# ScalarE applies the first norm four slots later in a software-pipelined vision tower

## The reference, cut to what matters

```python
def reference(x, ...):
    h = tok(x)                              # conv1, conv2, conv3, a layernorm ahead of each and a last one, then @ out_w
    h = h + attn(_layernorm(h, axis=-1))    # the "first norm"
    h = h + ffn(_layernorm(h, axis=-1))     # top-1 of 32 experts

def _layernorm(x, axis=-1, eps=1e-05):
    m = jnp.mean(x, axis=axis, keepdims=True)
    v = jnp.var(x, axis=axis, keepdims=True)
    return (x - m) / jnp.sqrt(v + eps)

# in attn: q, k, 8 heads, 64 wide
s[b, s, t, h] = -sum_w |q[b, s, h, w] - k[b, t, h, w]| / sqrt(64)    # softmax over s and one zero row; two value products
```

## Time and profile before

| | |
|---|---|
| median of three runs | 3510.13 us (3503.67 to 3510.3) |
| the profiled execution, its own time | 3508.91 us |
| its span, first to last instruction | 3507.0 us |
| mean granted TensorE clock | 0.986 |
| busy: PE / DVE / ACT / POOL | 92% / 88% / 78% / 81% |

### The profile page before, as it was taken

How to read it: one execution, slowest core, us unless ns; L and a number is a source line. 1 busy time by engine, 2 the same in 40 slices (tenths; PEclk the granted TensorE clock), 3 DMA queues, 4 the chain that set the end, 5 groups by cost and what they waited for, 6 DMA issues and landing times. The chain is left out here.

```text
span 3507.0 us, 78749 instructions
## 1 busy us (share of the span) xinstructions
PE 3243.3 (92%) x23140; PEld 2458.9 (70%) x23140; DVE 3086.9 (88%) x4389; ACT 2723.1 (78%) x4859; POOL 2856.5 (81%) x2792
## 2 busy tenths in 40 slices
PE   8899999999999999999999999999999999999888
PEld 6676777776777777677767777766777777777555
DVE  5888889998898989988999889989989999989886
ACT  3777787887787877877788878778778788777875
POOL 2888888888888888888888888878888888888885
PEclk8999999999999999999999999999999999999999
DMA  6778777787787787777888877877777887778884
GB/s 135 154 153 164 155 155 153 157 162 156 151 163 154 157 161 158 158 150 153 161 160 159 160 153 156 164 149 157 157 155 157 166 159 157 154 158 160 163 159 86
DMA packets 199653, 543.63 MB, mean 155 GB/s; under 512 B 69142, under 2 KB 133398, under 8 KB 146744
## 3 DMA queue, kind: packets, MB, share of 16 engines
q0 software_dynamic: 73728, 501.51, 72.0%
q1 hardware_dynamic: 125880, 41.54, 5.9%
HBM read 10.93 MB, written 2.10 MB: 4 GB/s over the span
## 5 line engine op out<-in xcount | busy, mean ns | idle before, releaser
L925 DVE TENSOR_REDUCE S<-psU 128x16 f32<-128x1024 f32 x2183 | 2604.4, 1217 | 297.8 <-PE psU L486 281.3
L486 PE MATMUL psU<-flat,kT 99*128 99x256 bf16 x16384 | 2304.1, 275 | 212.5 <-ACT absd L711 102.9
L711 ACT ACTIVATE absd<-psU 128x1024 f32<-128x1024 f32 x1913 | 1936.7, 1023 | 554.3 <-PE psU L486 541.0
L486 PEld LDWEIGHTS psU<-flat,kT 99*128 99x128 bf16 x16384 | 1495.6, 98 | 855.2 <-DVE S L925 219.3
L1194 POOL TENSOR_TENSOR absd<-absd 128x1024 f32<-128x1024 f32 (+2 forms) x512 | 1179.8, 2304 | 248.9 <-DMA absd<-absd 245.0
L1198 POOL TENSOR_TENSOR absd<-absd 128x512 f32<-128x512 f32 (+2 forms) x512 | 610.3, 1192 | 40.2
L1183 POOL DMA_DIRECT2D absd<-absd x512 | 454.2, 887 | 200.4 <-ACT absd L711 145.2
L1201 POOL TENSOR_TENSOR absd<-absd 128x256 f32<-128x256 f32 (+2 forms) x512 | 351.7, 687 | 40.1
L498 PE MATMUL psC<-c1in,w 128*128 128x384 f32 (+1 forms) x930 | 309.4, 415 | 0.8 <-DVE c1in L969 0.8
L590 PE MATMUL psZ<-P,v 128*128 128x256 f32 x1024 | 288.6, 384 | 0.0
L517 PE MATMUL psC<-c3in,w 128*128 128x128 f32 x1240 | 251.8, 287 | 1.7 <-DVE c3in L969 1.7
(11 more groups left out here) (180 smaller groups left out, 2231.3 us busy)
## 6 DMA issues: line engine op xcount, KB each, us to landing
absd<-absd POOLq DMA_DIRECT2D x412, 1024.0 KB, 7.9
absd<-absd POOLq DMA_DIRECT2D x65, 768.0 KB, 6.5
flat<-qparts SPq DMA_DIRECT2D x3072, 8.0 KB, 4.1
absd<-absd POOLq DMA_DIRECT2D x35, 512.0 KB, 4.9
xin<-in_x SPq DMA_DIRECT2D x32, 192.0 KB, 8.0
flat<-pattern SPq DMA_DIRECT2D x4, 768.0 KB, 10.9
out_h<-result SPq DMA_DIRECT2D x32, 64.0 KB, 6.0
w<-in_w SPq DMA_DIRECT2D x1, 1280.0 KB
```

What stands on the lines that cost most here:

```text
L486: mm = nc.tensor.matmul(psU[:, slot % PLACES, m], kT[0:ROWS + 3, b, m, :], flat[0:ROWS + 3, half % HALVES, :, lo:lo + BLOCK], start=True, ...
L711: nc.scalar.activation(absd[:, c % GROUPS, :, u], psU[:, slot % PLACES].rearrange("p (n a) s w -> p n (a s w)", n=2), ACT.Abs).then_inc(a_ ...
L925: nc.vector.tensor_reduce(S[:, b, hd, SB * c:SB * c + SB], psU[:, slot % PLACES].rearrange("p a s w -> p s a w"), AX.XY, ALU.add, apply_ab ...
```

## The change

```diff
-NORM_AT = dict(stat=4, rstd=4, x=6, turn=36, part1=29, rest1=26, part2=33, part3=34, hx=87)
+NORM_AT = dict(stat=4, rstd=4, x=10, turn=36, part1=29, rest1=26, part2=33, part3=34, hx=87)
```

## The result

| | before | after |
|---|---|---|
| median, 13 runs each on one chip | 3504.78 us (3496.59 to 3510.3) | 3495.69 us (3487.08 to 3504.39) |
| ratio, 95% interval | | 0.9973 [0.9963, 0.9984] |
| profiled execution: its own time, span | 3508.91, 3507.0 us | 3491.3, 3489.5 us |
| its mean granted clock | 0.986 | 0.994 |

The change makes the kernel faster by 9.1 us, 0.27%; the forecast was 12.0. The time forecast, 3498, lies only 2.3 us above the measured one by luck: the median of 13 runs of the kernel before is 5.4 us under that of the three runs from which I had started.

What follows compares the result with a forecast made beforehand. No engine is full, so waits between engines set the end. The terms -19.2 + 5 + 3.7 - 1.5 = -12.0 us take 3508.91 to 3496.9; with 1.2 us to the median, 3498 us; range 3485 to 3509 (forecast's own 3490 to 3503).

Steps and rivals of the forecast that it cites:

- The bound and the four passes: Waits between engines set the end; four passes with a clock fall at slot 11 lose their whole 19.18 us excess.
- the wait and 0.41 us: Before slot 11: TensorE's gap exceeds ScalarE's wait for nmrn by 0.41 us.
- GpSimd stays late: After slot 6 GpSimd stays late by the former wait, 6.2 us over four passes, owing ScalarE nmre at slot 67.
- the lateness at slot 67: First term: GpSimd's lateness comes out at slot 67 and is lost there; 5 us taken, bounds 0 and 6.2.
- one new fall: Second term: the gap at slot 67 makes the clock fall in one of four passes, 3.7 us; bounds none and four.
- The small passes: All passes beside the four: small waits and quiet-pass gains mostly turn up at slot 67; 1.5 us gain taken.
- the upper bound of 7.9: Most the other passes could gain: 4.4 us of small waits plus 3.5 us from quiet passes.
- the quiet passes' 0.54 us: At slot 11 TensorE can start 0.54 us earlier, mostly stopped by full VectorE; a quarter, 0.14 us, taken in 25 passes.
- the two terms: Losses at slot 67 set against the 19.2 us: 5 us of lateness and 3.7 us for one new clock fall.
- What is late next: Step asking where GpSimd's remaining lateness shows: at slot 67 on nmre, costing 5 us and 3.7 us.
- My -12: Whole kernel: the forecast sum of -12.0 us, taken from the profiled execution of 3508.91 us; chance 0.52.

Runs made afterwards that it cites:

- e2: The change plus ScalarE's wait for nmrn put back at slot 6, the two activations staying at slot 10; 3497.24 us, 0.9972 of the kernel before.
- e3: The change plus two unread 128x64 copies on ScalarE at slot 6, without a wait; 3497.35 us, 0.9979 of the kernel before.
- e10: The change with SyncE's image load behind the 15th group of query rows in place of the 4th; 3482.72 us, 0.9930 of the kernel before.
- e4: The change with SyncE's image load behind the 23rd group of query rows in place of the 4th; 3482.39 us, 0.9933 of the kernel before.
- e7: The change plus both the wait for nmrn and two unread copies at slot 6, x1 at slot 10; 3497.6 us, 0.9986 of the kernel before.
- e1: The change with x1 at slot 8 in place of slot 10, half the move; 3499.8 us, 0.9978 of the kernel before.
- e5: The kernel before, x1 at slot 6, with the image load behind the 23rd group of query rows; 3494.24 us, 0.9972 of the kernel before.
- e8: The change with the image load behind the 23rd group and the second norm's activations at slot 68, not 67; 3506.56 us, 1.0006 of the kernel before.

## Why the prediction came out as it did

**The bound and the four passes: right.** The falls behind slot 11 went as written, with 18.3 us by slot 24 against the 19.2 that I took; no gap over 1 us stands before slot 11 in these passes. That they come back with the wait alone is what e2 showed. I had put the gap down to the wait and 0.41 us; e2's smaller gaps say that x1's own work is part of it, and no run tells how much of the falls hangs on that part.

**GpSimd stays late: right in size by luck, wrong in place.** I took 5 us for the lateness at slot 67 and 3.7 for one new fall, 8.7 together. The four passes gave back 8.4 (18.3 won, 10.0 kept). But the most of it stood at slots 24 to 36, 5.8 us, on transfers of query rows, for which I had no term; only 1.6 at slots 64 to 80, and no fall. Two errors met there. The wait at L854 grew from 6.2 to 9.9 us, and in two passes one sees what I had described (timeline of the pass at 804.24, and the window behind it):

```profile
860.17 0.77 ACT L854 ACTIVATE x<-h,nmre,rstde 128x64 f32<-128x64 f32 x2 [1.51 <-POOL nmre L1222]
861.55 0.32 PE L607 MATMUL psZ<-ident,x 128*128 128x128 f32 x1 [1.76 <-ACT v L819]
```

```profile
861.50:871.50 10.00, 9.10 (x64) 7.00 (x65) 7.76 (x16) 7.13 (x10) 9.61 (x10) 1.00 0.77 153
```

Here the wait and the gap are longer than in the earlier trace rows (1.24, 1.49), and the clock stays up, which brought the profile 3.1 us in this pass that my sum did not have. In the same place of the same pass the clock fell in e3 (gap 1.53) and e10 (1.74) and stayed up in e4 (1.57). So one new fall in four passes was no bad term; that this profile has none is luck.

**The small passes: the failed term.** I wrote -1.5 for all other passes. Early they gained 7.0 us, near the upper bound of 7.9; of the quiet passes' 0.54 us, 0.16 got through, where I took 0.14. But it was given back at slot 36 as well, and the sum over the 24 passes beside the four and the one above is +0.3. The profiles' 17.6 are then 10.0 in the four passes, 3.1 in the one above and 4.8 in the lead-in, the first and the last passes, less this 0.3. I had forecast 10.5 for the first of these (19.2 less the two terms) and 1.5 for all other passes; that the 29 passes together come to 12.7, near my 12.0, is owed to the 3.1. The step that fell short is "What is late next": it named one place, and did not ask for TensorE's own wait on `flat`, 10.2 us, which was in the same view as the earlier trace rows. In this profile the next loss was 25 slots on, not 60.

**The clock over many runs.** The profiles held five falls in the loop before and one, in the pass before the last, after. Over all runs the mean clock went from 0.9875 to 0.9918; 0.0043 at 2.08 us for 0.001 is 9.0 us, of 10.4 between the means. So by this rate nearly the whole gain goes with fewer falls, and it is 9 and not 17.6 because the profile before had a clock below its kernel's mean (0.986) and that of after one above (0.994). This rate is no law, though: e2 and e7 are 7.7 us faster than the kernel before, of which it gives 3.9 and 1.8. My -12 came from an execution whose clock lay 0.0015 under the mean, as much as one fall of 10 us. With one of the four falls less, and its share of the lateness and of the new falls, the sum would have been about -9; that is an estimate.

**Left open.** Why GpSimd is late in the same passes in both kernels: `nmrn` comes 6.6, 6.0 and 6.5 us into the passes at 163.92, 1547.72 and 2292.88, and 6.5, 6.0 and 6.5 into those at 167.26, 1560.01 and 2307.31 before. Why slots 32 to 36 give back 11.9 us in the change, 5.6 in e3 and 0.3 in e1, which all come early. And what decides whether a gap brings a fall: over all profiles one fall stands behind a gap of TensorE of only 0.96 us (e5, at 1247.26), and none behind one of 2.47 us (e3, at 222.92). "TensorE: Matmul & The Clock Gate" of the Trainium skill, section "What's actually happening", has the monitor out of step with the kernel; it tells of the clock's rise at the start of matmul work, and that falls vary in the same way is my inference. The twin gaps of e8 agree with it, but no run here moved the phase.

## What to carry to other kernels

Price a late operand by what the clock does behind the gap and by what the delayed engines will meet next: of 25.4 us won by slot 24, 12.7 were left at the end of the passes. Before forecasting from an early gain, read every wait of the full engines, not just the one that the change removes; here another one, at slot 36, was worth as much as the change (about 10 us in the kernel before, 11 to 13 on top of the change). Where a kernel's time and mean clock vary together, compare clocks over all runs as well: they told the wait from its absence when the times could not. And measure a control before you lean on it: copies of x1's shape took half of x1's time.

## What I had not expected of the hardware

A 192 KB load behind the small pieces of the same queue took 8.1 us behind the 4th group of them and 2.5 us behind the 15th or the 23rd, and in the first place the 8 KB pieces were late for TensorE by 0.9 us in the shown pass; why is not shown. Two gaps of 1.38 us at the same instruction had the granted clock at 0.50 behind the one and 1.00 behind the other; 4.5 us of pass time hang on it, and the gap itself costs no more than 0.2. Two activations of 128x64 took 0.77 us with a scale and a bias from other tiles (x1), and 0.40 us as plain copies.
